# Second router of a fused MoE, mixer and MoE kernel: copies before normalising, a chunk normalised between two one-hots, tables behind the indices, idle products

## What is computed

```python
x = L0_attn_T                                          # (1, 4096, 256)
x = x + 0.5 * ffn(layernorm(x))
x = x + attn(layernorm(x))
x = x + 0.5 * ffn(layernorm(x))

def ffn(x):                                            # 8 experts, H = 256, I = 512, top 2
    gate_scores = softmax(x @ Wg)
    topk_scores, topk_idx = top_k(gate_scores, 2)
    topk_scores = topk_scores / (topk_scores.sum(-1, keepdims=True) + 1e-08)
    gate, value = einsum('bsh,ehi->bsei', x, W11), einsum('bsh,ehi->bsei', x, W12)
    fused = gate * sigmoid(gate) * value
    expert_out = einsum('bsei,eih->bseh', fused, W2)
    return sum_k(topk_scores[k] * expert_out[topk_idx[k]])
```

## Time and profile before

| | us |
|---|---|
| three executions | 986.29, 987.40, 987.94 |
| their median | 987.40 |
| the profiled execution, its own time | 985.32 |
| its span, first to last instruction | 983.5 |
| PE busy in it | 903.3 (92%) |
| mean granted PE clock, share of full | 0.962 |

### The profile page before, as it was taken

How to read it: one execution, slowest core, us unless ns; L and a number is a source line. 1 busy time by engine, 2 the same in 40 slices (tenths; PEclk the granted TensorE clock), 3 DMA queues, 4 the chain that set the end, 5 groups by cost and what they waited for, 6 DMA issues and landing times.

```text
span 983.5 us, 19046 instructions
## 1 busy us (share of the span) xinstructions
PE 903.3 (92%) x5396; PEld 778.3 (79%) x5399; DVE 582.7 (59%) x1394; ACT 391.2 (40%) x768; POOL 575.8 (59%) x605
## 2 busy tenths in 40 slices
PE   7769999999999999949897996899999999999994
PEld 6658888888888888827775874688888888888883
DVE  3986565675665655556726887555555555555551
ACT  3644244343443433325443775133333333333331
POOL 3435565666666665357514651577777777777762
PEclk9979999999999999968999996899999999999997
DMA  9654525526336281086202555654433333333332
GB/s 313 204 179 138 205 69 189 185 75 205 131 126 203 94 267 56 28 267 193 65 1 85 162 179 176 214 139 77 78 55 75 54 74 75 53 75 53 54 46 25
DMA packets 83936, 121.50 MB, mean 124 GB/s; under 512 B 12944, under 2 KB 62736, under 8 KB 83888
## 3 DMA queue, kind: packets, MB, share of 16 engines
q1 hardware_dynamic: 45376, 57.88, 18.1%
q0 software_dynamic: 24992, 37.32, 17.5%
q10 hardware_dynamic: 13520, 25.70, 7.7%
HBM read 73.62 MB, written 47.25 MB: 123 GB/s over the span
## 4 chain that ended last, share of the span: by engine, by line
PE 76%; DVE 7%; DMA 5%; ACT 5%; POOL 3%; issue 3%; ACTq 1%; SPq 0%; POOLq 0%
PE bank L1456 40%; PE bank L1479 20%; PE bank L1465 6%; PE bank L1448 3%; PE bank L1577 3%; ACT work L879 1%; DMA seq<-xt 1%; PE bank L1635 1%; DMA seq<-x_rows 1%; PE bank L1625 1%; ACT work L812 1%; ACT work L870 1%; DMA out_rows<-yb,idx_i 1%; PE bank L1394 1%; DMA seq<-y_rows 1%
## 5 line engine op out<-in xcount | busy, mean ns | idle before, releaser
L1165 DVE TENSOR_TENSOR sg<-sg,bank 128x512 f32<-128x512 f32 x142 | 97.7, 688 | 282.7 <-ACT sg L741 282.7
L1456 PE MATMUL bank<-w_hi,xt_hi 128*128 x568 | 237.8, 419 | 4.5 <-DVE xt_lo L1154 4.4
L1456 PE MATMUL bank<-w_hi,xt_lo 128*128 x568 | 225.1, 396 | 0.0
L1456 PE MATMUL bank<-w_lo,xt_hi 128*128 x568 | 225.0, 396 | 0.0
L733 ACT ACTIVATE yb<-bank,gates_in 128x256 f32<-128x256 f32 x142 | 67.3, 474 | 313.8 <-PE bank L1479 276.0
L551 POOL DMA_INDIRECT xg<-xn_rows,idx_i x142 | 140.1, 987 | 72.6 <-issue 41.4
L555 POOL DMA_INDIRECT gates_in<-gate_rows,idx_g x142 | 136.2, 959 | 48.0 <-issue 42.7
L1479 PE MATMUL bank<-w_hi,ft_hi 128*128 x568 | 160.3, 282 | 2.2 <-ACT yb L733 2.2
L1479 PE MATMUL bank<-w_lo,ft_hi 128*128 x568 | 160.5, 283 | 0.0
L1479 PE MATMUL bank<-w_hi,ft_lo 128*128 x568 | 160.4, 282 | 0.0
L565 POOL DMA_INDIRECT out_rows<-yb,idx_i x71 | 114.9, 1619 | 63.2 <-ACT yb L733 53.4
(11 more groups left out here) (289 smaller groups left out, 1293.8 us busy)
## 6 DMA issues: line engine op xcount, KB each, us to landing
w_lo<-w_lo_rows SPq DMA_DIRECT2D x32, 512.0 KB, 4.6
w_lo_rows<-w_lo ACTq DMA_DIRECT2D x16, 512.0 KB
xn_rows<-work SPq DMA_DIRECT2D x14, 512.0 KB, 3.4
seq<-y_rows SPq DMA_DIRECT2D x10, 512.0 KB, 5.2
x_all<-x SPq DMA_DIRECT2D x8, 512.0 KB, 9.0
w_lo_rows<-in_sb ACTq DMA_DIRECT2D x16, 256.0 KB, 2.4
gate<-x SPq DMA_DIRECT2D x16, 256.0 KB, 5.8
seq<-w ACTq DMA_DIRECT2D x7, 512.0 KB, 4.5
```

The source lines that it names most:

```text
L1165: nc.vector.tensor_tensor(sg[p], sg[p], ps_g[p][:], ALU.mult).then_inc(f_step, 1)
L1456: last = nc.tensor.matmul(dst[p][:], xt[p][:, c, :], of(w), start=(c == 0 and n == 0), stop=(c == DC - 1 and n == len(parts) - 1))
```

## The change

ACT: `rows_t(7)` now stands in step 7 of the loop, ahead of `norm_x2(5)`, instead of in step 8; `norm_x2(7)` leaves the place ahead of the one-hots and stands between those of groups 1 and 2. DVE, both rounds: `ends_of` and the part of `indices` behind `slots_ready` (now `tile_tables`) come after the indices; the gates' products with the reciprocal root (`in_units`) stay ahead of the indices in round 0 and go behind the tables in round 1. PE: six idle products in both rounds behind the waits for `slots_ready` and `tiles_ready`, ahead of the first tile, and five ahead of the last chunk's logits in the second router.

```diff
             def tiles_by_p(r):
                 for n in range(NQB):
+                    if r == 1 and n == 2:
+                        norm_x2(NCH - 1)
                     act.wait_ge(oh_ready, r * NQB + n + 1)
...
             for i in range(NCH + 1):
-                if i >= 1:
+                if 1 <= i < NCH:
                     rows_t(i - 1)
                 if i >= 2:
                     variance_x2(i - 2)
+                if i == NCH - 1:
+                    rows_t(NCH - 1)
...
             variance_x2(NCH - 1)
-            norm_x2(NCH - 1)
             tiles_by_p(1)
...
                     link(nc.vector.tensor_scalar(in_t, row_1, L - 1, None, ALU.bitwise_and))
                     nc.vector.tensor_tensor(idx_i[:], in_t, pad, ALU.add).then_inc(slots_ready, 1)
+
+            def tile_tables(r):
+
+                row_of = idx_s if r == 0 else row_1
                 link(nc.vector.reduce_sum(past_ends, past_end, AX.X))
...
-                ends_of(sorted_)
                 lg, second = logits[:], pair_gates[:, 1, :]
                 nc.vector.tensor_tensor(second, vals[:, :, 1], vals[:, :, 0], ALU.subtract)
                 link(nc.vector.tensor_tensor(lg, lg, vals[:, :, 0:1].to_broadcast([P, NT, E]), ALU.subtract))
-                dve.wait_ge(rstd_ready, NCH if r == 0 else 3 * NCH)
-                nc.vector.tensor_tensor(second, second, rstd_of, ALU.mult)
-                nc.vector.tensor_tensor(lg, lg, rstd_of.unsqueeze(2).to_broadcast([P, NT, E]), ALU.mult).then_inc(below_max, 1)
+
+                def in_units():
+
+                    dve.wait_ge(rstd_ready, NCH if r == 0 else 3 * NCH)
+                    nc.vector.tensor_tensor(second, second, rstd_of, ALU.mult)
+                    nc.vector.tensor_tensor(lg, lg, rstd_of.unsqueeze(2).to_broadcast([P, NT, E]), ALU.mult).then_inc(below_max, 1)
+
+                if r == 0:
+                    in_units()
                 indices(r)
+                ends_of(sorted_)
+                tile_tables(r)
+                if r == 1:
+                    in_units()
...
                 turn = 2 * XG
+                keep_busy(ps_g[0][:], before.unsqueeze(1).to_broadcast([P, G, P]), 6)
                 rows_in(0, 0)
...
             ranks_of(1, NCH - 2)
+            keep_busy(ps_g[0][:], before.unsqueeze(1).to_broadcast([P, G, P]), 5)
             logits_2(NCH - 1)
```

More of the change, by code:

```diff
@@ L1033, in indices @@
                 if r == 0:
-                    row_of = idx_s
                     dve.wait_ge(norm_act, NCH // 2)
@@ L1038, in indices @@
                 else:
-                    row_of = row_1
-                    link(nc.vector.scalar_tensor_tensor(row_of, token, -1.0, pad, ALU.add, ALU.add))
+                    link(nc.vector.scalar_tensor_tensor(row_1, token, -1.0, pad, ALU.add, ALU.add))
                     nc.vector.tensor_scalar(pad, inv_p, 0.0, float(L), ALU.is_equal, ALU.mult)
-                    link(nc.vector.tensor_scalar(in_t, row_of, L - 1, None, ALU.bitwise_and))
+                    link(nc.vector.tensor_scalar(in_t, row_1, L - 1, None, ALU.bitwise_and))
                     nc.vector.tensor_tensor(idx_i[:], in_t, pad, ALU.add).then_inc(slots_ready, 1)
+            def tile_tables(r):
+                row_of = idx_s if r == 0 else row_1
                 link(nc.vector.reduce_sum(past_ends, past_end, AX.X))
```

## The result

| | before | changed |
|---|---|---|
| median, first comparison (4 executions each) | 987.62 | 980.31 |
| ratio, 95% interval | | 0.9938, 0.9921 to 0.9956 |
| median, second comparison, another chip (27 and 11) | 987.05 | 983.05 |
| ratio, 95% interval | | 0.9964, 0.9950 to 0.9978 |
| profiled execution, its span | 983.5 | 978.7 |

The change is faster by 7.3 us in the first comparison and by 4.0 in the second; the profiled executions stand 4.8 apart. 2.2 were forecast. I hold the changed kernel to be 4 to 5 us faster: the two intervals have 0.9950 to 0.9956 in common, and the two profiled executions differ by 4.8.

A forecast was written before the change was run, and what follows sets the result against it. TensorE carries 76% of the span, so only the routers could move: second router 3.3 us gained, first 1.05 lost, net 2.2 faster, median 985.2 us. Range of 8 in 10: 982.3 to 988.3.

The forecast's parts named there:

- what the clock gives back: First tiles: a warm start from the idle products gains 0.4 us in the second round, nothing in the first.
- The copies ahead of normalising, with the five idle products: Second router's last logits: earlier copies less the five products' cost gain 0.4 us, range -0.7 to 2.0.
- Normalising moved: ACT, second router: first one-hot scaled without waiting for the last normalising, gain 2.07 us, with over 2 us to spare.
- Tables behind the indices: DVE, second router: tables and gates' products after the indices, gain 0.15 us.
- Gather and six idle products: Second router, gather to first transposes: the gather shares less with the load beside it; transposes start 0.3 us better.
- First router: DVE there has no slack, so tables behind the indices delay the first tile: loss 1.05 us.
- signs that I had named as right: One-hot scaled within 0.2 of DVE's; second router's gather about 2.6 earlier; first router's first tile 1.0 later, DVE last.
- sign of being wrong: PE waiting longer than DVE, store releasing the gather, later logits, or first tiles' products at 0.23 each from the start.
- rival 1: First tiles of both rounds: idle products keep the clock up; net -4.8, 982.6 us; chance 0.19.
- Rival 2: Second router: the later store of the last rows holds POOL's gather; net about 0 to -0.8, 987.0 us; chance 0.18.
- rival 3: PE's queue, both routers: idle products run at half clock and PE comes late; net +0.9, 988.3 us; chance 0.15.

The follow-up runs named there:

- e1: The changed kernel without all eleven idle products; 994.61 us, ratio 0.9966 to the kernel before.
- e2: The changed kernel without the five idle products ahead of the last logits, the six kept; 993.50 us, ratio 0.9950 to the kernel before.
- e5: The kernel before with only the two moves on ACT (copies and last normalising); 982.99 us, ratio 0.9957 to the kernel before.
- e12: The kernel before with only the last chunk's copies moved ahead of normalising chunk 5; 987.31 us, ratio 1.0003 to the kernel before.
- e13: As e10 with four more idle products between each first tile's transposes and its first product; 980.93 us, ratio 0.9930 to the kernel before.
- e4: The kernel before, unchanged, run again for a second profile; 999.72 us, ratio 1.0016 to the kernel before.
- e14: As e10 but without the six idle products in the second router; 982.15 us, ratio 0.9949 to the kernel before.
- e3: The changed kernel without the six idle products ahead of each first tile, the five kept; 995.54 us, ratio 0.9970 to the kernel before.
- e9: The kernel before with only DVE's new order in both rounds; 987.91 us, ratio 1.0008 to the kernel before.
- e10: The changed kernel with the first router's tables put back ahead of its indices; 981.03 us, ratio 0.9951 to the kernel before.
- e11: The changed kernel once more, on another chip; 983.05 us, ratio 0.9964 to the kernel before.
- e17: As e10 without the five idle products and with expert 3's low-part load moved behind the gates' store; 979.86 us, ratio 0.9926 to the kernel before.
- e15: The kernel before with only the load of expert 3's low parts moved behind the store of the gates; 984.75 us, ratio 0.9977.
- e6: The kernel before with only the last normalising moved between the second and third one-hot; 985.31 us, ratio 0.9974 to the kernel before.
- e16: As e6 with the load of expert 3's low parts also moved behind the store of the gates; 982.37 us, ratio 0.9948 to the kernel before.

## Why the prediction was wrong

The direction and the mechanism on ACT were right, the size was not: 2.2 forecast, 4.8 between the traces, 4.0 and 7.3 in the medians. The step that failed first is the term for the copies with the five idle products ahead of the logits; the second is what the clock gives back. Of the about 2.6 between 2.2 and 4.8, the second router brings 2.8 (6.1 instead of 3.3: 1.9 at the logits, 1.2 by the clock, the rest small) and the first 0.9 (0.1 lost instead of 1.05), and 1.2 are lost elsewhere. By the steps of the sum:

- **The copies ahead of normalising, with the five idle products: 0.4 forecast, 2.3 measured.** This is the largest miss, and it lies just outside the upper end that I gave (2.0). Without the five products the copies alone have the logits start 1.6 earlier, at 2.3, and they take 2.8 to 3.4 instead of 3.6, because part of them still falls in the full clock (e1, e2, e5, e12): ends at 5.1 to 5.7. I had the start right (587.4), then laid the five on top of it, half of the products at half clock, which ate the gain in my sum. They ran at full clock, and so did the logits behind them; in e13 alone the clock was down, and there my lower end is close (7.7, 0.1 later than before). At full clock the five cost 1.1 and give 0.9 to 1.6; the gain is the move's own.
- **Normalising moved: 2.07 forecast, 2.0 measured** (4.3 at the first scaling less 2.3 at the logits). That 2 us of slack hide it was right as well. What I didn't see is that the two moves on ACT need each other, so that e12 gives nothing.
- **Tables behind the indices: 0.15 forecast in the second router, nothing measured.** The gather goes out 2.0 behind the last router product in both. (From the first scaling to the gather 0.2 is even lost: the last products took 2.05 instead of 1.42.)
- **Gather and six idle products: 0.3 forecast, 0.5 measured,** as two larger things: 1.3 to 1.6 from the gather going out ahead of expert 3's load (from its issue to PE ready 4.7 before, 3.4 in e5, 3.0 in e1; in e4, issued late enough, it was 3.4 too), of which the six take 0.6 to 1.1 (e5, e14, e1 against the changed kernel). I had written that it "would share less of its time with the load that runs beside it today", and then priced it as a spread, 3.2 to 4.5. It comes nearer to a step: the rows move ahead of the load, or behind nearly all of it.
- **What the clock gives back: 0.4 forecast, 0.3 up to the first product and 1.3 behind it measured** (the stretch between the first two tiles, 5.4 to 4.1). Against e1 and e3, though, which have no six, they are worth 0.4 to 0.6 net, and e4 had the 1.3 without them: most of this term is luck of the profile of before. On the page on TensorE: Matmul & The Clock Gate, section "What's actually happening", of the Trainium skill: that activity releases the clock is borne out in part, and that it differs from run to run is borne out fully (e2 and the changed kernel, where nothing differs in the first router: 2.94 and 1.67 for its first tile's products).
- **First router: 1.05 lost forecast, 1.3 measured at the first product** (6.30 against 5.00), shown by e9 and taken back by e10. I had put the clock at nothing here. Where it was full, only 0.1 of the loss was left at the second tile; where it wasn't, 1.1 to 1.4 (e2, e9).

Of the signs that I had named as right, DVE's one-hot, the place of normalising and DVE as the last in the first router came; the first router products came 4.3 nearer instead of 2 to 3 and the gather 4.1 earlier instead of 2.6. One sign of being wrong came too: the first tiles ran at full clock from the start. So rival 1's event did happen, in this profile and in e11, at 1.0 in the first router and 0.4 to 0.6 net in the second by the runs without the six. That is about 1.5 of the 2.6 that it added; that its total is the 4.8 of the traces is chance, since the logits' 1.9 are not in it and 1.2 were lost elsewhere. (Its time was 982.6; the lower end of the range, said to be its middle, stands at 982.3.) Rival 2 is not seen in the changed kernel, where DVE released the gather; in e17 the store did release it (last row below), at 26.2 instead of about 25.1. The first half of rival 3 occurs in e13: the five ran at half clock. Its price was too high: the logits ended 0.1 later than before, not 0.7, the gather still went out 1.2 earlier, and the six were at full clock again.

```profile
611.49 1.10 POOL L551 DMA_INDIRECT xg<-xn_rows,idx_i  x1 [11.32 <-DMA xn_rows<-work]
```

Open are the 7.3 of the first comparison: four executions each, with an interval from 4.3 to 7.8, of which the trace shows 4.8. What the other 2.5 are no run shows.

## What to carry to other kernels

Price a step that goes earlier twice: once by its time, and once by what it now comes ahead of, on PE the fall of the clock and on the DMA engines the next bulk load; neither shows in the duration of the step itself. Where two waits lie in series on one in-order engine, removing the first alone may earn nothing (e12) and both together all, so undo a change part by part before calling a part useless. Behind the latency-bound start of a stage, issue bulk loads after the small transfer that everyone waits for (e15: 2.8 us between the medians, 1.2 of it seen in the trace).

## What had not been expected of the hardware

- A 1 MB load issued about when the gather is holds back its 128 rows: 5.7 us from issue to use in e6 with the load beside it, 3.0 in e16 without.
- Five idle products ahead of the logits cost about as much as they give where the clock is up (logits end at 5.1 to 5.7 without, 5.2 with), and take 2.1 us where it is down (e13).
- The same kernel twice gave 0.16% between medians with an interval that leaves out 1 (e4).
